# Filler matmuls ahead of five waits of TensorE in a vision tower with a state-space layer

## What is computed

```
h = patches(x, 16x16) @ W.T + b                      # 196 tokens of 256
h = layernorm(h + state_space(h))                    # 512 inner channels, 16 states
h = layernorm(h + token_shift_ffn(h))
h = layernorm(h + attention(h))                      # 8 heads, 4-wide queries and keys
h = layernorm(h + experts(h))                        # 8 experts, the best 2 of them weighted

def state_space(x):                                  # A = -exp(A_log)
    xb, z = split(x @ in_proj_w.T)
    xb = silu(conv4(xb));  dt_in, Bp, Cp = split(xb @ x_proj_w.T)
    dt = softplus(dt_in * dt_w + dt_b)
    h[t] = exp(dt[t] * A) * h[t-1] + xb[t] * dt[t] * Bp[t]
    y = sum_states(h * Cp) + xb * D
    return (layernorm(y) * ln_g + ln_b) * silu(z) @ out_w.T
```

## Time and profile before

| | |
|---|---|
| median of 3 executions | 5539.83 us (5514.9 to 5540.97) |
| the profiled execution | 5522.53 us |
| its span, first to last instruction | 5520.7 us |
| mean granted TensorE clock | 0.917 |
| TensorE busy | 4738.8 us, 86% |
| GpSimd busy | 4455.6 us, 81% |
| ACT busy | 3925.5 us, 71% |
| VectorE busy | 3737.4 us, 68% |

### The profile page before, as it was taken

One profiled execution on the slowest core, in us unless ns is written; L12 is line 12 of the kernel. 1 busy time (PEld: TensorE's weight loads), 2 busy tenths in 40 slices (PEclk: granted clock), 3 DMA queues, 4 the chain that ended last, 5 costly groups with the idle time before them and its releaser, 6 DMA issues.

```text
span 5520.7 us, 91938 instructions
## 1 busy us (share of the span) xinstructions
PE 4738.8 (86%) x31488; PEld 4137.2 (75%) x31488; DVE 3737.4 (68%) x7504; ACT 3925.5 (71%) x9282; POOL 4455.6 (81%) x3336
## 2 busy tenths in 40 slices
PE   4788889888888888888888888888888888888887
PEld 3677777777777777777777777777777777777776
DVE  3667666667677667667677677676776776766663
ACT  4777777777777777776777777777776777776752
POOL 4988888888888888888888888888888888887860
PEclk7889989999999999999999999999999999999887
DMA  4222222222222222222222222222222222222110
GB/s 105 63 47 60 68 55 56 71 50 61 67 54 61 66 56 61 61 60 61 55 67 61 55 64 64 55 62 66 55 62 66 55 58 69 55 57 70 41 39 24
DMA packets 730609, 328.76 MB, mean 60 GB/s; under 512 B 631543, under 2 KB 655393, under 8 KB 729889
## 3 DMA queue, kind: packets, MB, share of 16 engines
q1 hardware_dynamic: 730144, 322.89, 24.0%
HBM read 307.88 MB, written 14.90 MB: 58 GB/s over the span
## 4 chain that ended last, share of the span: by engine, by line
DVE 35%; PE 26%; ACT 26%; issue 9%; POOL 3%; SPq 1%; DMA 0%; DVEq 0%; ACTq 0%; POOLq 0%
DVE X L1070 14%; PE G L699 8%; ACT dA L873 6%; PE YB L579 4%; DVE xbs L1047 3%; DVE nmx L1117 3%; PE SB L658 3%; PE G L619 2%; PE G L671 2%; ACT dt L854 2%; ACT soft L854 2%; ACT y L888 2%; DVE hg L1186 2%; ACT pT L952 2%; ACT pr L937 2%
## 5 line engine op out<-in xcount | busy, mean ns | idle before, releaser
L1070 DVE TENSOR_TENSOR_SCAN X<-dA,X 128x392 f32<-128x392 f32 x2048 | 1875.7, 958 | 1203.7 <-ACT dA L873 1165.0
L474 POOL TENSOR_TENSOR X<-X,Cb 128x784 f32<-128x784 f32 x1024 | 1894.7, 1850 | 4.2 <-DVE X L1070 4.2
L464 POOL TENSOR_TENSOR X<-u,Bb 128x784 f32<-128x784 f32 x1024 | 1895.3, 1851 | 2.2 <-DMA Bb<-proj_rows 2.1
L873 ACT ACTIVATE dA<-dt,negA 128x195 f32<-128x195 f32 x4096 | 1524.0, 417 | 303.3 <-DVE X L1070 263.5
L579 PE MATMUL YB<-idn,X 128*98 128x128 f32 x8192 | 1152.7, 289 | 33.3 <-POOL X L474 33.3
L579 PEld LDWEIGHTS YB<-idn,X 128*98 128x98 f32 x8192 | 973.6, 136 | 138.4 <-POOL X L474 116.8
L699 PE MATMUL G<-hg,we 128*128 128x196 f32 x4096 | 771.9, 348 | 49.8 <-DVE hg L1186 49.6
L699 PEld LDWEIGHTS G<-hg,we 128*128 128x128 f32 x4096 | 730.3, 203 | 61.1 <-issue 58.4
L556 PE MATMUL SB<-hT,win 128*128 128x196 f32 x2048 | 454.9, 386 | 184.2 <-ACT pT L952 170.6
L556 PEld LDWEIGHTS SB<-hT,win 128*128 128x128 f32 x2048 | 415.4, 226 | 214.0 <-ACT hT L808 192.3
L671 PE MATMUL G<-vs,pT 98*98 98x33 f32 x4096 | 428.0, 262 | 130.7 <-DVE att L1134 113.0
(11 more groups left out here) (147 smaller groups left out, 7379.4 us busy)
## 6 DMA issues: line engine op xcount, KB each, us to landing
Bb<-proj_rows SPq DMA_DIRECT2D x256, 392.0 KB, 4.4
Cb<-proj_rows SPq DMA_DIRECT2D x256, 392.0 KB, 3.8
Gb<-gate_rows SPq DMA_DIRECT2D x64, 784.0 KB, 4.7
px<-in_x SPq DMA_DIRECT2D x1024, 36.8 KB
out<-ob SPq DMA_DIRECT2D x64, 196.0 KB
dtin<-proj_rows SPq DMA_DIRECT2D x64, 98.0 KB, 2.8
we<-in_w_e SPq DMA_DIRECT2D x1, 2048.0 KB
proj_rows<-pj SPq DMA_DIRECT2D x64, 25.3 KB
```

The source lines that it names most:

```text
L464: tt(X[(GROUPS * s + g) % RING][:], u[q % 2][:, c:c + 1, :].broadcast_to([P, NG, T]), Bb[:, NG * ng:NG * (ng + 1), :], ALU.mult).then_inc( ...
L474: tt(t[:], t[:], Cb[:, n0:n0 + NG, :], ALU.mult).then_inc(prod_ready, 1)
L873: last = go(dA[i % DRING][:, j, 1:T], dt_[q % 2][:, c, 1:T], ACT.Exp, scale=negA[:, c, n:n + 1])
L1070: v.tensor_tensor_scan(t, dA[i % DRING].rearrange("p n t -> p (n t)"), t, 0.0, ALU.mult, ALU.add).then_inc(scan_done, 1)
```

## The change

It defines two helpers that issue matmuls whose result nobody reads. `keep_busy` multiplies the identity with a slice of the weights win and adds into the unused columns of YB; it waits for nothing. `keep_busy_in` does the same into a bank that it is given: here the bank of "qk", so it waits until that bank's use before, "AV2", has been drained. The helpers are called at five slots, once an image each, 22 matmuls in all.

```diff
+WARM_AV, WARM_H2T, WARM_XB, WARM_SCORES, WARM_PAIR = 5, 4, 6, 4, 3
...
+            def keep_busy(n):
+
+                for _ in range(n):
+                    mm(YB[0:TB, BLK * P:BLK * P + T], lhsT=idn[:, 0:TB], rhs=win[:, 0, 0:T], start=False, stop=False,
+                       skip_group_check=True)
+
+            def keep_busy_in(o, n):
+                for _ in range(n):
+                    mm(o[:, 0:T], lhsT=idn[:], rhs=win[:, 0, 0:T], start=True, stop=True)
...
+                    for s, q in at(13):
+                        keep_busy(WARM_PAIR)
                     for p in range(PAIRS):
                         for s, q in at(AT_PAIR[p]):
                             expert_pair(s, p)
...
                             patches(s, part)
+                    for s, q in at(5):
+                        keep_busy(WARM_AV)
+                    for s, q in at(12):
+                        keep_busy(WARM_SCORES)
                     for n in range(UNITS):
                         for s, q in at(AT_SCORES[n]):
                             scores(s, n)
...
+                    for s, q in at(AT_QK - 1):
+                        keep_busy_in(free("qk", s), WARM_XB)
                     for s, q in at(AT_XB):
                         pe.wait_ge(where["embed"].drained, where["embed"].count("embed", s))
                         project_in(s, hT[q], "xb", 0)
...
+                    for s, q in at(8):
+                        keep_busy(WARM_H2T)
                     for s, q in at(AT_H2T):
                         pe.wait_ge(normed["ffn"], s + 1)
                         turn(s, "h2T", h2[q % 2])
```

## The result

| | before | with the change |
|---|---|---|
| median | 5540.4 us (5514.9 to 5551.01) | 5462.55 us (5461.19 to 5464.71) |
| ratio | | 0.9866, 95% interval 0.9833 to 0.99 |
| the profiled execution | 5522.53 us | 5463.63 us |
| mean granted TensorE clock | 0.917 | 0.963 |

The change makes the kernel 1.3% faster. 5436 us was forecast, with a range of 5375 to 5490. Between the two profiled executions the gain is 59 us, where the sum had 87. Between the medians it is 78 us, because the profiled execution of before lay 18 us under its median.

The account below looks back on a forecast made before the run. TensorE was taken to be short of work and of clock, the clock losing 2.47 us an image. 81.00 plus 1.0 gives 82.0 us an image, 1.47 under 83.47; times 59 is 87 us off 5522.53: 5436 us, range 5375 to 5490.

Parts of the forecast that it names:

- 81.00 us: An image at 2.4 GHz throughout: shortest halves 48.18 and 32.82 us added, against the mean of 83.47.
- The second part: VectorE's period from L1060 to the next L1055, holding the attention and projection waits; claimed about 32.8 us in nearly every image.
- Rival 1: Transposes behind the attention don't hold the clock; that half stays at 33.94 us, 1.12 over the shortest: 5502 us, chance 0.07.
- overhang: Fillers before the h2 transpose and projection take 3.38 us against one 2.80 us wait, sticking out by 0.58.
- The scores' wait: TensorE's wait before L648, 3.88 us behind a full-clock projection; 1.95 us were to stay idle after the fillers.
- one image in two: Share of images taken as still slowed by the clock behind the scores.
- price of 2.0 us: Cost of an image slowed behind the scores: the middle of 1.49 and 2.50 us, thus 1.0 us an image.
- first part: VectorE's period from L1055 to L1060, holding the scores and experts waits; 48.2 us in about half the images, 50 or more otherwise.
- the two periods added for the end: Two periods for images still in work after 5162.89 us, making 59 periods of 1.47 us saved.
- Rival 2: The scores' wait always slows the clock: 83.0 us an image, 28 us saved, 5495 us, chance 0.12.
- The fillers before the experts: Three before L699: 1.01 us hidden in a 1.26 us wait at full clock, on the path at half clock.
- The transposes behind the attention: Some 7 us of transposes and narrow matmuls behind L671, taken to hold full clock, as 5.2 us of such work ran at 1.00.

Follow-up runs that it names:

- e1_sc10: The change with ten fillers before the scores instead of four: 5389.75 us, ratio 0.9735 to the kernel before.
- e3_av_only: The change with only the five fillers before the attention, the other seventeen left out: 5440.14 us, ratio 0.9826 to the kernel before.
- e10_lean: The change with five fillers before the attention, ten before the scores and none elsewhere: 5394.14 us, ratio 0.9719 to the kernel before.
- e2_no_pair: The change without the three fillers before the experts: 5443.9 us, ratio 0.9835 to the kernel before.
- e5_fit: The change with five fillers before the attention, eight before the projection, eleven before the scores, none elsewhere: 5384.95 us, ratio 0.9734 to the kernel before.
- e9_sc7: The change with seven fillers before the scores instead of four: 5399.45 us, ratio 0.9731 to the kernel before.
- e8_turns_sc10: The change with ten fillers before the scores and fourteen transposes replacing the five matmuls before the attention: 5413.71 us, ratio 0.9784 to the kernel before.
- e6_sc10_no_av: The change with ten fillers before the scores and none before the attention: 5459.44 us, ratio 0.9869 to the kernel before.

## Why the prediction was right, and where it was off

**The loss is the clock, and 81.00 us is an image without it.** Right: 80.98 in e1_sc10.

**The second part is given back in whole.** Right: 32.81 us, slowed in none of 57 images, where before had 51. It is also all that the change gains, as e3_av_only shows. The four images of the prediction made this gain look smaller than it is: their mean second part is 33.94 us, that of all 57 is 34.43, so 1.61 of the 2.47 us lost to the clock lay in the second part. The sum isn't touched by it, since it starts from the mean of all periods. Rival 1 is: its price of 1.12 us should have been 1.61.

**No time from the h2 and projection fillers past their wait.** Right in the sum. Their overhang, put at 0.58 us, was 0.20: wait and fillers before the scores come to 2.35 + 1.33 = 3.68 against 3.88. The new wait on the drain of AV2 did not come up. What the sum passed over is what these ten fillers do to the wait behind them: they keep it at its full 3.88 us in every image, while behind a slow projection it was some 2.2 us. A short fall at the projection costs nothing by itself (e3_av_only, e10_lean), and with all fillers but the three before the experts the kernel is no faster than with the five before the attention alone (e2_no_pair, e3_av_only).

**The scores' wait.** 1.95 us were to stay idle, and 2.36 did. The step that failed is "one image in two": it was every image, 57 of 57. One in two was not a bad reading of before, where the clock fell behind 20 of 44 waits of 2.0 to 2.8 us; it did not carry over. The price of 2.0 us was too high: with the second part at 32.81, the mean first part is 82.43 - 32.81 = 49.62, so 1.44 us over the shortest, just under the lower end of 1.49. It is made up otherwise than was thought. In 48 of the 57 images the slow stretch is short; in the 14 such images of before the first part was 48.52 us, 0.3 over the shortest, and here it is 49.35, because the three fillers stand in it. Only nine have a long one. Chance times price was 1.0 and came out at 1.44. This 0.43 over 57 periods is 25 us, and with the 3 us of the two periods added for the end it is the whole miss of 28. Rival 2 (always slowed, chance 0.12) had the mechanism, with a price too high. The two errors have opposite signs, and it is luck that they partly cancel: by the same sum, every image slowed at 2.0 us would have been 5495.

**The fillers before the experts** were taken as hidden at full clock and on the path at half. Both are so: 0.26 us of wait left in e1_sc10, and L710 1.1 us later in the change. The upper end of the price had them in.

**The transposes behind the attention** were held to keep the clock, on the evidence of one stretch at 1.00. In the changed kernel they do, behind fillers that are matmuls. As fillers they do not always. The forecast came out right with a reason that was too simple: a stretch at full clock shows that the clock had not fallen yet, not that its work would have kept it.

**What stays open** is why every image of the change is slowed at the scores, while 19 are not in e2_no_pair, with the same fillers ahead of them. The trace of the change shows a pattern: in the eight images from 1474.41 the granted clock over the 4 us from the start of the scores is 0.50, 0.70, 0.67, 0.64, 0.61, 0.58, 0.57, 0.57, and at 2133.08 it is 0.52 and the row begins again. So the slow stretch slides slowly against the scores from image to image. It looks as if the clock were set at moments of its own, and an image of 82.1 us met them in nearly the same place as the one before. No run tested that.

## What to carry to other kernels

Where TensorE is on the path and its granted clock falls behind a wait, matmuls that nobody reads are worth putting into that wait, up to the end of the wait and no further: here five were worth 70 us, six more in another wait 73, and four past the end of that wait cost 29. Not every wait is worth it: without fillers before the projection the median was only 4 and 9 us higher (e10_lean against e1_sc10 and e5_fit), and the ratio no worse. A wait filled only in part can cost more than it gives, if the clock falls all the same. Find which fall costs by cutting a period at marks on another engine and comparing slowed and unslowed images of the same trace. Leave the slack behind such a wait empty, since it is what takes up the next delay, and don't steer by TensorE's busy share or its mean clock alone.

## What the runs showed of the hardware

- Filler matmuls of 196 columns start 0.332 us apart at full clock (1.33 us for four), a little under the 0.338 of L547.
- How often the granted clock fell behind the scores went with the idle time before them: with 0.36 us idle in none of 57 images (e1_sc10), with 1.38 in 3 of 57 (e9_sc7), with 2.0 to 2.8 in 20 of 44 (before), with 3.88 in 13 of 13 (before) and 25 of 25 (e3_av_only). It is not decided by that alone: with 2.35 us it fell in 38 of 57 images of e2_no_pair and in all 57 of the change.
- Transposes as fillers keep the full clock in some images and not in others: behind them the second part was slowed in 30 of 57 images (e8_turns_sc10), behind matmuls of about the same length in 3 (e1_sc10), with nothing there in 53 (e6_sc10_no_av).
- Two kernels with the same mean granted clock, 0.963 (the change) and 0.962 (e10_lean), are 68 us apart: a slow stretch costs by where it stands.
- Writing fillers into unused columns of a bank that ACT drains in the same slots shows no cost: the first and second part are 48.16 and 32.82 us with 28 fillers an image, and the shortest of before were 48.18 and 32.82.
